# TensorE's order inside an odd half step: the value products ahead of the score unit for the maxima

## The chip, the cores and the metric

The kernel runs on one core of one Trainium2 chip. The metric is the device time of one execution in microseconds (us). The median of three runs of the kernel before is 2089.74 us (2085.26 to 2090.35).

## The reference, cut to what matters

Two transformer layers with adaptive layer norm run over x of shape 8 x 1024 x 128 (eight batches). Layer 0 has a causal attention with one head and a mixture of eight experts. Layer 1 has an attention with 16 heads of width 8 and a feed-forward part. The part around the change is layer 1's attention:

```python
q = jnp.einsum('bnc,hc->bnh', x, Wq).reshape(b, n, m, d)   # m = 16 heads, d = 8
k = jnp.einsum('bnc,hc->bnh', x, Wk).reshape(b, n, m, d)
v = jnp.einsum('bnc,hc->bnh', x, Wv).reshape(b, n, m, d)
weight = jnp.einsum('bimd,bjmd->bmij', q * scale, k * scale)
weight = jax.nn.softmax(weight, axis=-1)
a = jnp.einsum('bmij,bjmd->bimd', weight, v).reshape(b, n, m * d)
```

There are 8 x 16 heads, each with 1024 x 1024 scores, and each row of scores needs its maximum before the exponentials.

## The kernel before, in words

**The units.** Layer 1's scores are computed twice. A *unit of the maximum* (`max_scores`, L613) is a pair of matmuls, one for each head of a pair of heads: 128 queries against 512 keys, 48 rows of bf16 parts. VectorE reduces it to row maxima (`row_max`, L1023). A *unit of the exponential* (`exp_scores`, L623) is the transposed product, 128 keys against 512 queries, with three more rows that bring in the negated maxima. ScalarE takes its exponential into one of four tiles `p` (L810). The *value products* (`values`, L639) are eight matmuls in the profile (four heads and halves in fp32) that multiply the exponentials of two units by v, and add them up in the bank `pv_psum`.

**The half steps.** The main loop counts half steps h. In half step h the exponential's unit h and the maximum's unit h + 32 are filled (LEAD is 16 steps, so the maxima run two pairs of heads ahead). There are 64 pairs of heads and 16 half steps to each, so 1024 half steps. Two half steps, an even one and the odd one behind it, are called a step here. In odd half steps the value products of the step before are issued as well. Every engine runs through the same half steps in its own program.

**The buffers.** All units, of both kinds, take turns in three PSUM buffers of two banks each, in the order exponential h, maximum h + 32, exponential h + 1, and so on. A unit may be filled once the unit three places ahead of it is emptied (`buffer_of`). So exponential h waits for VectorE's reduction of the maximum's unit filled in half step h - 2, and the maximum's unit of half step h waits for ScalarE's exponential of unit h - 1. The value products in odd half step h need the exponentials of the units up to h - 2.

**The rest of the work.** Everything else (layer 0's attention and experts, the projections, the feed-forward part, called *fills* here when they are TensorE's) is cut into stages, and a planner (`lay_out`, L149) puts them into half steps: `ROOM = (13, 4)` gives each even half step 13 and each odd one 4 units of room, `WORK` has each stage's size, and at most one fill goes into a half step. In a half step each engine issues its stages behind its unit. All fills share one bank, `side_psum`; a fill waits until ScalarE (`side_act`) or VectorE (`side_dve`) has emptied the one before. TensorE's program for a half step before the change is:

```python
            if 0 <= h < PAIRS * UNITS:
                exp_scores(h)
            if h + 2 * LEAD < PAIRS * UNITS:
                max_scores(h + 2 * LEAD)
            if h > 1 and h % 2:
                values(h // 2 - 1)
            for name, *at in plan.get(h, ()):
```

The program of TensorE (`tensor_program`, L402) stands here with its helpers. Other lines that the steps below touch: L711 to L800 are ScalarE's stages, L738 its exponential of layer 0 (`exp0`), L928 and L930 VectorE's softmax of layer 0, L852 and L855 the layer norm's statistics, L945 and L951 the search for the largest gate, and L1128 GpSimd's mask.

Of the kernel before, what the change touches and what calls it, by code (L numbers as in the profile page):

```python
# [266 lines left out]
def build(nc, ctx, x_in, Wq0, Wk0, Wvdown, Wvup, Wg, bg, We, be, c0, wmod0,  # L267
# [102 lines left out]
    def halves(half):  # L370

        return slice(4 * half, 4 * half + 4), slice(half * BANK, (half + 1) * BANK)
# [8 lines left out]
    def maxima_in(pair):  # L381
        return S[f"maxima{pair % 2}"], 2 * 16 * (pair // 2 + 1)
# [14 lines left out]
    def rows_of(hh, count):  # L397
        return slice(ROW_HALF * hh, ROW_HALF * hh + count)
# [3 lines left out]
    def tensor_program():  # L402
# [9 lines left out]
        def emptied(*key):  # L412
            u = side[key]
            pe.wait_ge(S["side_" + u.by], u.emptied)
# [186 lines left out]
        def buffer_of(kind, n):  # L601
            buffer, before = unit(kind, n)
            if before:
                pe.wait_ge(S[before[0] + "_done"], before[1] + 1)
            return buffer

        def max_scores(n):
            pair, i, half = n // (2 * T), n // 2 % T, n % 2
            slot, of = pair // GROUP % SLOTS, pair % GROUP
            buffer = buffer_of("max", n)  # L610
            pe.wait_ge(*operands(pair // GROUP))
            for hh in range(2):
                m = e.matmul(buffer[:, hh, :], q_ops[rows_of(hh, K_MAX), slot, of, i * P:(i + 1) * P],  # L613
                             k_ops[rows_of(hh, K_MAX), slot, of, halves(half)[1]], start=True, stop=True)
            m.then_inc(S["max_filled"], 1)

        def exp_scores(n):
            pair, kb, half = n // (2 * T), n // 2 % T, n % 2
            slot, of = pair // GROUP % SLOTS, pair % GROUP
            buffer = buffer_of("exp", n)  # L620
            pe.wait_ge(*maxima_in(pair))
            for hh in range(2):
                m = e.matmul(buffer[:, hh, :], k_ops[rows_of(hh, K_EXP), slot, of, kb * P:(kb + 1) * P],  # L623
                             q_ops[rows_of(hh, K_EXP), slot, of, halves(half)[1]], start=True, stop=True)
            m.then_inc(S["exp_filled"], 1)

        def values(step):
            pair, kb = divmod(step, T)
            b, hp = divmod(pair, HEADS // 2)
            if kb == 0:  # L630
                pe.wait_ge(S["pv_zero"], 1)
                pe.wait_ge(S["pv_copied"], pair)
                emptied("v1", b, 1)
                pe.wait_ge(S["v1_ones"], 2)
            pe.wait_ge(S["exp_done"], 2 * step + 2)
            for hh in range(2):
                for half in range(HALVES):
                    q = 32 * (2 * hh + half)
                    m = e.matmul(pv_psum[q:q + VW, :], v1[b % 2][:, kb, 2 * hp + hh, :], p_sb[(2 * step + half) % 4][:, hh, :],  # L639
                                 start=kb == 0, stop=kb == T - 1)  # L640
            m.then_inc(S["pv_done"], 1)
# [7 lines left out]
        for h in range(-2 * LEAD, PAIRS * UNITS + 2):  # L649
            if 0 <= h < PAIRS * UNITS:  # L650
                exp_scores(h)
            if h + 2 * LEAD < PAIRS * UNITS:
                max_scores(h + 2 * LEAD)
            if h > 1 and h % 2:
                values(h // 2 - 1)
            for name, *at in plan.get(h, ()):
                if name in stages:
                    stages[name](*at)
# [564 lines left out]
    def sync_program():  # L1223
# [132 lines left out]
        for half in range(2):  # L1356
            sp.wait_ge(S[f"out{half}"], 32 * (B // 2))
            sp.wait_ge(S[f"parts{half}"], 16 * PRODUCTS * B)

    tensor_program()  # L1360
    scalar_program()
    vector_program()
# [27 lines left out]
```

## Time and profile before

| what | value |
| --- | --- |
| median of three runs | 2089.74 us |
| the profiled execution's own time | 2084.8 us |
| its span (first to last instruction) | 2083.3 us |
| its mean granted TensorE clock | 0.962 |
| PE busy | 1748.1 us (84%) |
| DVE busy | 1521.8 us (73%) |
| ACT busy | 1354.4 us (65%) |
| POOL busy | 772.0 us (37%) |
| main loop with both kinds of unit | about 237 to 2014 us of the span |

PE is TensorE, PEld its weight loads, DVE VectorE, ACT ScalarE and POOL GpSimd. A busy time counts an engine as busy from the start of an instruction to its modelled end; matmuls overlap, so TensorE's busy time is more than the issue slots that it uses. A wait row says which engine and line sat idle, and whose instruction ended the idle time.

### The profile page before, as it was taken

The page shows a single profiled execution, that of the slowest core. Times are in us where ns is not written, and L with a number is a line of the kernel's source. Part 1 is how long each engine was busy: PE and PEld are TensorE (multiplying, and loading weights), DVE is VectorE, ACT ScalarE, POOL GpSimd, SP SyncE. Part 2 cuts the span into 40 slices and gives each one's busy share as a digit, 9 for nine tenths or more (in the row PEclk, how much of TensorE's full clock was granted, in tenths as well). Part 3 has the DMA queues.
Part 4 walks back from the last instruction along what each step waited for, and adds up shares of the span by engine and source line. Part 5 has one row for each costly group of instructions (what it writes and reads, how often), then busy time and mean ns, then how long its engine had stood idle before and what let it go on. Part 6 is the DMA issues. An engine that isn't in the chain of part 4 may idle for free.

```text
span 2083.3 us, 31153 instructions
## 1 busy us (share of the span) xinstructions
PE 1748.1 (84%) x11854; PEld 666.5 (32%) x11854; DVE 1521.8 (73%) x2300; ACT 1354.4 (65%) x1826; POOL 772.0 (37%) x1127
## 2 busy tenths in 40 slices
PE   5574799988989899998989889898989989777784
PEld 3453332333323243233333333233333333112112
DVE  3435877787777876778768886778868787888861
ACT  2332377766777767776767767776767766766673
POOL 4572245314543164333543155432543243302000
PEclk9886799999999999999999999999999999999997
DMA  2004012112020212002221121302112021301101
GB/s 59 21 21 111 22 40 80 29 38 62 24 86 21 62 54 86 28 20 62 60 63 29 31 61 48 90 20 62 34 33 76 21 59 50 90 20 47 26 15 36
DMA packets 83140, 98.79 MB, mean 47 GB/s; under 512 B 11600, under 2 KB 52784, under 8 KB 82992
## 3 DMA queue, kind: packets, MB, share of 16 engines
q1 hardware_dynamic: 82992, 96.81, 17.0%
q8 instruction: 94, 1.54, 0.3%
q14 instruction: 54, 0.44, 0.1%
HBM read 61.25 MB, written 34.73 MB: 46 GB/s over the span
## 4 chain that ended last, share of the span: by engine, by line
PE 60%; ACT 16%; DVE 12%; POOL 6%; issue 4%; SPq 1%; DMA 1%; ACTq 0%; POOLq 0%; DVEq 0%
PE pv_psum L639 19%; ACT p L810 11%; PE buffer L613 8%; PE buffer L623 8%; DVE row_max L1023 7%; PE side_psum L418 3%; PE side_psum L537 3%; PE side_psum L489 3%; PE side_psum L542 3%; PE side_psum L512 2%; PE side_psum L505 2%; PE side_psum L495 1%; PE side_psum L465 1%; PE side_psum L548 1%; POOL rest L1128 1%
## 5 line engine op out<-in xcount | busy, mean ns | idle before, releaser
L1023 DVE TENSOR_REDUCE row_max<-buffer 128x2 f32<-128x1024 f32 x1024 | 1241.5, 1220 | 339.1 <-PE buffer L613 325.5
L810 ACT ACTIVATE p<-buffer 128x1024 f32<-128x1024 f32 x1024 | 1032.7, 1026 | 328.3 <-PE buffer L623 324.8
L639 PE MATMUL pv_psum<-p,v 128*9 128x512 f32 x4096 | 538.9, 598 | 4.4 <-ACT p L810 3.6
L613 PE MATMUL buffer<-k_ops,q_ops 48*128 48x512 bf16 x2048 | 397.9, 387 | 162.2 <-ACT p L810 130.5
L623 PE MATMUL buffer<-q_ops,k_ops 51*128 51x512 bf16 x2048 | 398.6, 388 | 36.8 <-DVE row_max L1023 34.5
L623 PEld LDWEIGHTS buffer<-q_ops,k_ops 51*128 51x128 bf16 x2048 | 97.4, 93 | 440.9 <-DVE row_max L1023 205.6
L613 PEld LDWEIGHTS buffer<-k_ops,q_ops 48*128 48x128 bf16 x2048 | 99.8, 95 | 268.7 <-ACT p L810 229.6
L1158 POOL TENSOR_SCALAR nm_parts<-nm 128x16 bf16<-128x16 f32 x64 | 13.2, 206 | 401.1 <-DVE nm L972 380.4
L1145 POOL TENSOR_TENSOR hm<-masks,hT_f 128x1024 f32<-128x1024 bf16 x64 | 136.6, 2144 | 57.3 <-PE side_psum L542 48.1
L1128 POOL TENSOR_SCALAR rest<-s 128x128 f32<-128x128 f32 (+3 forms) x64 | 137.1, 2142 | 5.7
L1126 POOL TENSOR_TENSOR s<-s,consts 128x128 f32<-128x128 f32 x64 | 29.2, 456 | 284.2 <-ACT s L732 284.2
L928 DVE CUSTOM_DVE_ANT_0 s<-s,rest 128x128 f32<-128x128 f32 (+3 forms) x64 | 56.1, 876 | 86.5 <-POOL rest L1128 86.5
L639 PEld LDWEIGHTS pv_psum<-p,v 128*9 128x9 f32 x4096 | 60.8, 88 | 163.7 <-issue 151.8
L738 ACT ACTIVATE s<-s,nm 128x256 f32<-128x256 f32 (+3 forms) x64 | 55.2, 863 | 70.8 <-DVE nm L930 70.8
L489 PE MATMUL side_psum<-hT,g 128*128 128x512 f32 (+2 forms) x158 | 72.8, 543 | 2.6
L745 ACT COPY p0T<-side_psum 128x512 f32<-128x512 f32 (+3 forms) x83 | 43.1, 519 | 48.0 <-PE side_psum L495 47.9
L537 PE MATMUL side_psum<-we,hm 128*128 128x128 f32 x448 | 65.8, 290 | 0.0
L542 PE MATMUL side_psum<-we,hm 128*128 128x128 f32 x448 | 64.9, 288 | 0.0
L542 PEld LDWEIGHTS side_psum<-we,hm 128*128 128x128 f32 x448 | 54.2, 191 | 31.0 <-issue 31.0
L495 PE MATMUL side_psum<-consts,s 128*128 128x128 f32 x278 | 49.5, 294 | 10.8 <-ACT s L738 6.7
L732 ACT COPY s<-side_psum 128x256 f32<-128x256 f32 (+3 forms) x79 | 37.7, 477 | 29.2 <-PE side_psum L489 28.3
L537 PEld LDWEIGHTS side_psum<-we,hm 128*128 128x128 f32 x448 | 55.0, 193 | 3.8
(245 smaller groups left out, 1833.6 us busy)
## 6 DMA issues: line engine op xcount, KB each, us to landing
masks<-masks_rows SPq DMA_DIRECT2D x16, 1024.0 KB, 5.6
products<-q_parts SPq DMA_DIRECT2D x48, 256.0 KB, 3.4
products<-k_parts SPq DMA_DIRECT2D x48, 256.0 KB, 3.8
q_ops<-products SPq DMA_DIRECT2D x64, 192.0 KB, 3.4
k_ops<-products SPq DMA_DIRECT2D x64, 192.0 KB, 4.2
attention<-o_sb SPq DMA_DIRECT2D x256, 18.0 KB
x<-in_L_attn_inputs SPq DMA_DIRECT2D x8, 512.0 KB, 3.9
w_sb<-in_L_ffn_W SPq DMA_DIRECT2D x16, 256.0 KB, 3.0
```

What stands on the lines that cost most here:

```text
L418: m = e.matmul(v[:, j * C:(j + 1) * C], weight(j), moving, start=True, stop=True)
L489: e.matmul(v[:, 0:w], g0[:, i * P:(i + 1) * P], hT0[:, at:at + w], start=True, stop=True).then_inc(S["side_filled"], 1)
L495: m = e.transpose(v[:, j * P:(j + 1) * P], s0[i % 2][:, k * P:(k + 1) * P], ident)
L537: e.matmul(o, hm[t % 2][:, k, :], we[:, k, :], start=False, stop=False)
L542: m = e.matmul(o, hm[t % 2][:, k, :], we[:, k, :], start=False, stop=k == EXPERTS - 1)
L613: m = e.matmul(buffer[:, hh, :], q_ops[rows_of(hh, K_MAX), slot, of, i * P:(i + 1) * P], k_ops[rows_of(hh, K_MAX), slot, of, halves(half)[ ...
L623: m = e.matmul(buffer[:, hh, :], k_ops[rows_of(hh, K_EXP), slot, of, kb * P:(kb + 1) * P], q_ops[rows_of(hh, K_EXP), slot, of, halves(half ...
L639: m = e.matmul(pv_psum[q:q + VW, :], v1[b % 2][:, kb, 2 * hp + hh, :], p_sb[(2 * step + half) % 4][:, hh, :], start=kb == 0, stop=kb == T - 1)
L810: e.activation(p_sb[n % 4][:, :, :], unit("exp", n)[0][:, :, :], ACT.Exp).then_inc(S["exp_done"], 1)
L1023: e.tensor_reduce(mx[pair % 2][:, :, i, half], unit("max", n)[0][:, :, :], axis=AX.X, op=ALU.max).then_inc(S["max_done"], 1)
L1128: e.tensor_scalar(rest[:, 0:n], s[:, P:P + n], 0.0, NEG, ALU.is_equal, ALU.mult).then_inc(S["masked"], 1)
L1145: e.tensor_tensor(hm[t % 2][:, :, :], masks[:, :, cols], hT_f[:, cols].unsqueeze(1).broadcast_to([C, EXPERTS, P]), op=ALU.mult).then_inc(S ...
```

## The change

In every half step TensorE's program now issues the value products directly behind the exponential's unit and ahead of the maximum's unit. Even half steps have no value products, so only odd ones differ. No instruction, wait, buffer or other engine's program is added or removed; the order of the units in the three buffers stays the same.

```diff
         for h in range(-2 * LEAD, PAIRS * UNITS + 2):
             if 0 <= h < PAIRS * UNITS:
                 exp_scores(h)
+            if h > 1 and h % 2:
+                values(h // 2 - 1)
             if h + 2 * LEAD < PAIRS * UNITS:
                 max_scores(h + 2 * LEAD)
-            if h > 1 and h % 2:
-                values(h // 2 - 1)
             for name, *at in plan.get(h, ()):
                 if name in stages:
                     stages[name](*at)
```

## Rows read from the trace of the kernel before

**Rows 1.** The page: busy time by engine, share of the span, instructions.

```profile
PE 1748.1 (84%) x11854; PEld 666.5 (32%) x11854; DVE 1521.8 (73%) x2300; ACT 1354.4 (65%) x1826; POOL 772.0 (37%) x1127
```

**Rows 2.** The waits: waiting engine and line, who ended it, total, times, longest.

```profile
PE buffer L613 <- ACT p L810: 130.5, 220, 1.0
...
PE buffer L623 <- DVE row_max L1023: 34.5, 56, 3.5
```

**Rows 3.** Groups by line: the units and value products (busy us, mean ns).

```profile
L1023 DVE TENSOR_REDUCE row_max<-buffer 128x2 f32<-128x1024 f32 x1024 | 1241.5, 1220 | 339.1 <-PE buffer L613 325.5
L810 ACT ACTIVATE p<-buffer 128x1024 f32<-128x1024 f32 x1024 | 1032.7, 1026 | 328.3 <-PE buffer L623 324.8
```

**Rows 4.** Timeline of a step without fills: start us, us, engine, line, operation.

```profile
2006.55 0.39 PE L623 MATMUL buffer<-q_ops,k_ops 51*128 51x512 bf16 x2
...
2007.00 0.38 PE L623 MATMUL buffer<-q_ops,k_ops 51*128 51x512 bf16 x2
2007.04 1.94 ACT L810 ACTIVATE p<-buffer 128x1024 f32<-128x1024 f32 x2 [0.93 <-PE buffer L623]
2007.20 2.58 DVE L1023 TENSOR_REDUCE row_max<-buffer 128x2 f32<-128x1024 f32 x2 [0.29 <-PE buffer L613]
2008.12 0.39 PE L613 MATMUL buffer<-k_ops,q_ops 48*128 48x512 bf16 x2 [0.74 <-ACT p L810]
2008.44 1.05 PE L639 MATMUL pv_psum<-p,v 128*9 128x512 f32 x8
2009.42 0.39 PE L623 MATMUL buffer<-q_ops,k_ops 51*128 51x512 bf16 x2
...
2009.87 0.38 PE L623 MATMUL buffer<-q_ops,k_ops 51*128 51x512 bf16 x2
```

**Rows 5.** Timeline, TensorE: units at which the counted kinds of step begin or end.

```profile
241.68 0.64 PE L613 MATMUL buffer<-k_ops,q_ops 48*128 48x512 bf16 x2
...
244.42 0.39 PE L623 MATMUL buffer<-q_ops,k_ops 51*128 51x512 bf16 x2
...
260.13 0.39 PE L623 MATMUL buffer<-q_ops,k_ops 51*128 51x512 bf16 x2
...
1925.81 0.39 PE L623 MATMUL buffer<-q_ops,k_ops 51*128 51x512 bf16 x2
```

**Rows 6.** Timeline, TensorE in an odd half step with a fill.

```profile
1005.55 0.39 PE L623 MATMUL buffer<-q_ops,k_ops 51*128 51x512 bf16 x2
1005.78 0.38 PE L613 MATMUL buffer<-k_ops,q_ops 48*128 48x512 bf16 x2
1006.09 1.04 PE L639 MATMUL pv_psum<-p,v 128*9 128x512 f32 x8
1007.06 1.16 PE L418 MATMUL side_psum<-wff,hT_b 128*128 128x128 f32 x8
1008.15 0.39 PE L623 MATMUL buffer<-q_ops,k_ops 51*128 51x512 bf16 x2
```

**Rows 7.** Timeline, VectorE and a late maximum's reduction in a stretch without fills.

```profile
949.38 1.21 DVE L1023 TENSOR_REDUCE row_max<-buffer 128x2 f32<-128x1024 f32 x1
...
951.04 1.21 DVE L1023 TENSOR_REDUCE row_max<-buffer 128x2 f32<-128x1024 f32 x1
...
952.30 0.39 PE L623 MATMUL buffer<-q_ops,k_ops 51*128 51x512 bf16 x2 [0.22 <-DVE row_max L1023]
```

**Rows 8.** Timeline, layer 0's negated maximum on VectorE and the exponential that uses it.

```profile
346.45 0.15 DVE L930 TENSOR_SCALAR nm<-mx 128x1 f32<-128x1 f32 x1
...
347.02 0.61 ACT L738 ACTIVATE s<-s,nm 128x384 f32<-128x384 f32 x1
```

**Rows 9.** Stretches: us, busy PE, PEld, DVE, ACT, POOL, PEclk, DMA share, GB/s.

```profile
243.00:2014.00 1771.00, 1567.16 (x10867) 553.71 (x10867) 1390.71 (x1954) 1249.34 (x1635) 649.93 (x975) 0.99 0.18 48
1868.00:2014.00 146.00, 110.84 (x826) 25.77 (x822) 124.89 (x125) 99.93 (x112) 16.94 (x43) 1.00 0.12 30
1061.00:1073.00 12.00, 7.79 (x40) 2.11 (x38) 5.26 (x9) 5.67 (x8) 5.00 (x14) 0.72 0.03 6
```

## The prediction

> **What bounds the kernel now.** I read the page first. TensorE is busy 84% of the span, VectorE 73%, ScalarE 65% [rows 1], so no engine is full, and the question is who waits for whom. In the loop TensorE is busy 1567 of 1771 us [rows 9]; what it idles is mostly one wait. The waits [rows 2] show it: before a maximum's unit (L613) TensorE sat idle 130.5 us in 220 waits for ScalarE, before an exponential's unit (L623) only 34.5 us for VectorE. The timeline shows the round that makes the first wait [rows 4]. In the even half step the exponential's unit starts at 2006.55; ScalarE takes it at 2007.04 and has two of them done 1.94 us later, the first after 1.03 [rows 3, 4]. The next odd half step's maximum's unit needs that buffer and starts only at 2008.12, where 2007.23 would have done: score units follow each other every 0.22 to 0.23 us when nothing holds them (1005.55 to 1005.78 [rows 6]; 2006.55 to 2007.00 is two of them). The value products stand behind this wait though their own exponentials were ready long before. The change lets them run in that hole.
>
> **What the change costs and brings.** No instruction and no semaphore is added: the value products need exponentials up to unit h - 2, for which the even half step's maximum's unit has already waited. So only the order counts. I work it out start to start, with e for the start of the odd exponential's unit.
>
> *Issue slots.* Before: unit to unit 0.23, maximum's unit to value products 0.31 (1005.78 to 1006.09), value products to whatever follows 0.97 to 0.98 (fill or score unit alike) [rows 4, 6]. The next work starts at e + 1.51 plus the wait w. Afterwards: value products at e + x, the maximum's unit 0.98 later, then 0.22 to a score unit or 0.31 to a fill. The step x, from an exponential's unit to value products, is not in the trace. It lies between 0.22 (score unit to score unit) and 0.31 (the other score unit to the same value products); I take 0.31, since both score units have nearly the same shape. So an odd half step without a fill costs 1.51 as before (-0.007), and one with a fill 1.60 (+0.084), because TensorE now goes twice from score units to full-height fp32 matmuls. Counted through the 494 steps from 241.28 to the last maximum's unit, 256 have an odd fill (first half step at 244.42, last at 1925.81) [rows 5]: together **+20 us**. With x at 0.22 the sum would be 0.09 x 494 = 43 us lower; with 0.05 more than 0.31, 25 us higher.
>
> The Trainium skill (TensorE: Matmul & The Clock Gate, The mechanism) says that a weight load is pulled ahead of running matmuls when its row group does not conflict or when it goes to the background weight buffer. By the second half of that rule the load for the value products would hide and x would be near 0.22, with the sum 43 us lower; the 0.31 between units and value products [rows 6] speaks against it.
>
> *The wait that goes.* w is what the odd maximum's unit is later than e + 0.227. It is more than the idle time, since the profile calls TensorE busy for 0.16 us of it. Over the same steps w is above 0.02 in 294 (first at 241.68, last at 2008.12 [rows 4, 5]), and sums to **-175 us**. Check against the waits: 130.5 + 220 x 0.163 = 166 [rows 2], the rest being small ones. Afterwards the unit comes at e + 1.29, where the buffer is free in all but a few steps.
>
> *The wait that comes.* The maximum's unit is now 1.06 - w later, and with it VectorE's reduction: 0.42 us from the unit's start (2006.55 + 0.23) to the reduction's at 2007.20, 1.22 for it, 0.06 (951.04 + 1.21 to 952.30, with rounding) to the next unit, 1.70 in all [rows 3, 4, 7]. The exponential's unit of the next odd half step needs that buffer. Without fills it would be issued 0.22 x 3 = 0.66 after the maximum's unit, and so now waits about 1.04. The round becomes: maximum's unit, reduction (1.70), exponential's unit, 0.31, value products, 0.98, maximum's unit: 2.99 us a step. Before, in rows 4, it was 2009.87 - 2007.00 = 2.87, and 2.79 at best. So a step without any fill gets longer by 0.1 to 0.2, in spite of the hole that is filled. With fills between (0.6 us or more) the new wait shrinks; with two it is nothing. Put step by step into the trace as max(0, maximum's unit's new start + 1.70 - next odd unit's new start), it is there in 183 steps (first before 244.42, 0.04 us; last before 2009.87) and sums to **+132 us**. By kind (w, slots, new wait): no fill in the odd half nor in the next even one, 109 steps (first at 260.13, last at 2007.00 [rows 4, 5]): -79 -1 +94; only the even fill, 129: -34 -1 +30; only the odd, 48: -25 +4 +7; both, 208: -37 +17 +0. First-order sum: -23.
>
> *What is late next.* (a) Where w goes, the following even units come earlier by w and meet ScalarE, whose second exponential still ends when it did (2007.04 + 1.94 = 2008.98 [rows 4], and the unit that needs it would be due at 2008.73), or VectorE. The same step-by-step max over these two gives **+14**. (b) VectorE may be late by itself. Its reductions at 949.38 and 951.04 are 1.66 apart, 0.44 of it other work of its own, and the unit at 952.30 waits for the second [rows 7]. There w is gained and lost again. With each reduction's measured end as a floor the sum rises by 8; part of that end was itself set by waits that go, so I take **+4**. (c) VectorE's stages in odd half steps start up to 1 us later: fills emptied by VectorE that have a fill right behind, +4; three exponentials of layer 0 that come one half step behind their softmax. In such a case the maximum is ready 0.42 us before its use (346.60 and 347.02 [rows 8]), and would now be ready about 0.4 late. Together **+6**. Work on GpSimd and the DMA queues is planned with half steps of slack and is not passed; I cost it at nothing. If it moved, it would be by a fraction of 1 us in each batch, as one wait of 3.5 us a batch for GpSimd's mask, in the stretch at 1061 [rows 9], would take in.
>
> Sum: -175 + 20 + 132 + 14 + 4 + 6 = **+1 us**, against the profiled execution's 2084.8 us. The median shown stands 4.9 us above that execution; the same difference put on it gives 2091 us. About 0.3% (6 us) is what a measurement of this kernel can tell from no change.
>
> **Rivals.**
>
> *The holes are filled and little comes behind (faster).* Terms (a) to (c) are guesses about cover. If they are nothing, 2090 - 23 = 2067; if x also is less than 0.31, each 0.01 takes 5 us more. For it: in the 256 steps with an odd fill the new wait is only 7 us against 62 us of w. Against: spots where VectorE is full anyway [rows 7]. Anything from 2067 to 2083 falls here.
>
> *VectorE becomes the round's bound (slower).* Place: the odd exponential's unit after a late reduction. In those 183 steps VectorE must now idle between its two reductions for about 0.54 us (2.99 - 2 x 1.22), at a fixed place. Its other work, 1391 us less two reductions of 1.22 in each of 495 steps, is 183 us in the loop [rows 3, 9], 0.37 a step, and comes in lumps. A lump above 0.54 lengthens the round by the excess, where before three buffers evened it out. If half of the 183 steps have a lump with 0.25 over, that is +23: 2113. It decides from about 6 us, so already at 25 such steps. For it: VectorE is busy 125 of 146 us in the last stretch [rows 9], where the loop has few fills. Against: many lumps lie in steps with fills.
>
> *The clock falls (slower).* The loop now runs at a granted 0.99 to 1.00 even in the last stretch, where TensorE waits in nearly each step; it fell to the lower of its two levels (1.2 for 2.4 GHz) only after an idle stretch of some 3.5 us [rows 9]. The new waits are about 1 us. If it fell in the last stretch alone, the round of 2.99 would grow by the value products' 1 us and two slots, to 4.2: +55 us, 2145. The Trainium skill (TensorE: Matmul & The Clock Gate, A second HAM failure mode: psum-queue depth-cycling) reports a clock that swings when TensorE idles briefly between groups; this trace has such idling without the swing.
>
> **Chances.** Forecast, within 0.3%: 0.42. Filled holes: 0.27. VectorE's round: 0.29. Clock: 0.02. The range reaches from the faster rival's middle, 2070, to most of the slower one's, 2110; within the forecast's own case it is 2085 to 2096.
>
> **What the changed profile would show.** The wait of L613 for ScalarE nearly gone (130.5 to under 15). L623's wait for VectorE up from 34.5 to some 120 to 160. Steps without fills at 2.99 or just above, from maximum's unit to maximum's unit. An odd half step with a fill like rows 6 at 2.69 instead of 2.60. The last stretch (1868 to 2014) 2 to 6 us longer, the batches in the middle shorter or the same. I am wrong if x is not 0.31, if VectorE sits idle in fewer places than before, or if ScalarE's waits grow by more than tens of us.

## The result and the profile after

The changed kernel takes 2104.5 us (median of five runs, 2100.9 to 2108.6) against 2088.5 us: a ratio of 1.008, 95% interval 1.0061 to 1.0099, so 13 to 21 us slower. The time lies inside the stated range of 2070 to 2110 us, but outside the 0.3% of the forecast, which was no change; the prediction gave this sign 0.31.

The page of the changed kernel, busy time by engine, then the chain (the work that ended last, followed back from the end) by engine and by line:

```profile
span 2102.0 us, 31153 instructions
PE 1767.2 (84%) x11854; PEld 679.9 (32%) x11854; DVE 1503.6 (72%) x2300; ACT 1364.8 (65%) x1826; POOL 775.6 (37%) x1127
...
PE 54%; DVE 27%; POOL 8%; ACT 6%; issue 4%; SPq 1%; DMA 1%; POOLq 0%; ACTq 0%; DVEq 0%
DVE row_max L1023 19%; PE pv_psum L639 17%; PE buffer L623 8%; PE buffer L613 7%; PE side_psum L537 3%; PE side_psum L489 2%; PE side_psum L542 2%; PE side_psum L495 2%; PE side_psum L418 2%; ACT p L810 2%; POOL rest L1128 1%; DVE s L928 1%
```

The chain of the kernel before, by engine:

```profile
PE 60%; ACT 16%; DVE 12%; POOL 6%; issue 4%; SPq 1%; DMA 1%; ACTq 0%; POOLq 0%; DVEq 0%
```

Busy shares are as before [rows 1], and say nothing of why it is slower. The chain does: ScalarE's share fell from 16 to 6% and VectorE's rose from 12 to 27%, of which its reductions are 19% (7% before). The kernel's waits and groups by line (idle time behind the second bar) show what was traded, against rows 2:

```profile
DVE row_max L1023 <- PE buffer L613: 403.3, 445, 18.5
...
PE buffer L623 <- DVE row_max L1023: 152.6, 215, 3.1
```

```profile
L613 PE MATMUL buffer<-k_ops,q_ops 48*128 48x512 bf16 x2048 | 400.5, 389 | 31.3 <-DMA k_ops<-products 21.4 <-DVE row_max L1023 8.2 <-ACT p L810 0.9
L623 PE MATMUL buffer<-q_ops,k_ops 51*128 51x512 bf16 x2048 | 398.4, 388 | 158.7 <-DVE row_max L1023 152.6 <-DMA q_ops<-nm_rows 1.5
```

The maximum's unit waited 130.5 us for ScalarE and now waits 0.9. The exponential's unit waited 34.5 us for VectorE and now waits 152.6, and VectorE itself idles 403 us for its units, in 445 waits, where it idled 325.5 [rows 3], in 491. The timeline of the changed kernel shows the round without fills, TensorE first, then VectorE:

```profile
2022.64 0.39 PE L613 MATMUL buffer<-k_ops,q_ops 48*128 48x512 bf16 x2
2022.86 0.38 PE L623 MATMUL buffer<-q_ops,k_ops 51*128 51x512 bf16 x2
2023.08 0.38 PE L613 MATMUL buffer<-k_ops,q_ops 48*128 48x512 bf16 x2
2024.35 0.39 PE L623 MATMUL buffer<-q_ops,k_ops 51*128 51x512 bf16 x2 [0.89 <-DVE row_max L1023]
2024.67 1.05 PE L639 MATMUL pv_psum<-p,v 128*9 128x512 f32 x8
2025.65 0.39 PE L613 MATMUL buffer<-k_ops,q_ops 48*128 48x512 bf16 x2
```

```profile
2023.07 2.36 DVE L1023 TENSOR_REDUCE row_max<-buffer 128x2 f32<-128x1024 f32 x2 [0.66 <-PE buffer L613]
2026.08 2.36 DVE L1023 TENSOR_REDUCE row_max<-buffer 128x2 f32<-128x1024 f32 x2 [0.66 <-PE buffer L613]
```

From the odd maximum's unit (2022.64) to the next odd exponential's unit (2024.35) are 1.71 us, then 0.32 to the value products and 0.98 to the next maximum's unit: 3.01 a step, where rows 4 had 2.87. VectorE's starts, 3.01 apart, say the same, and its 0.66 us of idle time in each step is the late unit seen from its side.

An odd half step with the fill of rows 6, in the changed kernel:

```profile
1013.84 0.39 PE L623 MATMUL buffer<-q_ops,k_ops 51*128 51x512 bf16 x2
1014.16 1.05 PE L639 MATMUL pv_psum<-p,v 128*9 128x512 f32 x8
1015.14 0.39 PE L613 MATMUL buffer<-k_ops,q_ops 48*128 48x512 bf16 x2
1015.46 1.16 PE L418 MATMUL side_psum<-wff,hT_b 128*128 128x128 f32 x8
1016.55 0.39 PE L623 MATMUL buffer<-q_ops,k_ops 51*128 51x512 bf16 x2
```

It takes 2.71 us instead of 2.60: two turns from score units to full-height matmuls (0.32 each) instead of one.

### The profile page after: what moved, and what is told of

Read it like the earlier page. It is cut to its first block, busy times and chain, and to the rows that moved or that the text cites. A ratio compares the mean times of both kernels' runs of the same rounds, so it can differ in the third digit from the quotient of the medians.

```text
span 2102.0 us, 31153 instructions
## 1 busy us (share of the span) xinstructions
PE 1767.2 (84%) x11854; PEld 679.9 (32%) x11854; DVE 1503.6 (72%) x2300; ACT 1364.8 (65%) x1826; POOL 775.6 (37%) x1127
## 4 chain that ended last, share of the span: by engine, by line
PE 54%; DVE 27%; POOL 8%; ACT 6%; issue 4%; SPq 1%; DMA 1%; POOLq 0%; ACTq 0%; DVEq 0%
DVE row_max L1023 19%; PE pv_psum L639 17%; PE buffer L623 8%; PE buffer L613 7%; PE side_psum L537 3%; PE side_psum L489 2%; PE side_psum L542 2%; PE side_psum L495 2%; PE side_psum L418 2%; ACT p L810 2%; POOL rest L1128 1%; DVE s L928 1%; PE side_psum L548 1%; PE side_psum L505 1%; PE side_psum L512 1%
## 5 line engine op out<-in xcount | busy, mean ns | idle before, releaser
L1023 DVE TENSOR_REDUCE row_max<-buffer 128x2 f32<-128x1024 f32 x1024 | 1226.4, 1218 | 405.1 <-PE buffer L613 403.3
L623 PE MATMUL buffer<-q_ops,k_ops 51*128 51x512 bf16 x2048 | 398.4, 388 | 158.7 <-DVE row_max L1023 152.6
L613 PE MATMUL buffer<-k_ops,q_ops 48*128 48x512 bf16 x2048 | 400.5, 389 | 31.3 <-DMA k_ops<-products 21.4
L613 PEld LDWEIGHTS buffer<-k_ops,q_ops 48*128 48x128 bf16 x2048 | 99.5, 94 | 505.7 <-issue 347.0
L1061 POOL TENSOR_SCALAR xn_f<-x,sm_f 128x128 f32<-128x128 f32 x112 | 52.3, 480 | 10.5 <-DVE k_parts L917 7.0
```

Of the source, the lines that this page charges most:

```text
L1023: e.tensor_reduce(mx[pair % 2][:, :, i, half], unit("max", n)[0][:, :, :], axis=AX.X, op=ALU.max).then_inc(S["max_done"], 1)
```

## The experiments

Theory A: the slowdown is the new round through VectorE, and the time lost depends on which odd half steps are changed. Theory B: it is the extra turns of the last fence. All runs were timed in the same rounds as the kernel before, and every ratio below is to that kernel.

**The change in some odd half steps only.** TensorE's loop gets a condition; `fill(h)` is the planner's size of the fill in half step h.

```diff
+        def fill(at):
+            return sum(work(s) for s in plan.get(at, ()) if s[0] in WORK or s[0].startswith("times_v"))
+
...
+            early = CONDITION
+            if h > 1 and h % 2 and early:
+                values(h // 2 - 1)
             if h + 2 * LEAD < PAIRS * UNITS:
                 max_scores(h + 2 * LEAD)
-            if h > 1 and h % 2:
+            if h > 1 and h % 2 and not early:
                 values(h // 2 - 1)
```

With `fill(h) > 0`:

> Value products ahead of the maximum's unit only in the 257 odd half steps that have a fill; the old order in the other 238. Theory A (the slowdown is the new round: maximum's unit, reduction, next odd exponential's unit, value products): the changed kernel's steps of this kind took 15.5 us less than before and the others 32 us more, so about 2073 us, faster than before. Theory B (the slowdown is the extra turn from score units to full-height matmuls, 0.084 us in each odd half step with a fill): all of these turns are kept and nothing else is, so slower than before, 2100 to 2110 us.

Measured 2069.1 us, ratio 0.989 (0.9877 to 0.9909): faster than before, with every extra turn in it. With `fill(h) == 0`, the complement:

> The complement: value products ahead of the maximum's unit only in the 238 odd half steps without a fill. Theory A: 2088.5 + 32 = about 2120 us, slower than the change itself (2104.5). Theory B: no extra turn at all, so no slower than before, 2088 us or less.

Measured 2111.8 us, ratio 1.010 (1.0085 to 1.0115). It adds no turn and is the slower one. Theory B falls as the whole cause: the turns cost, but the half steps that have them gain all the same, and the loss lies where there are none. A's size was 32 us and came out at about 21. The two halves together (-22 and +21) come to nothing, while the whole change costs 16, so they do not simply add.

With `fill(h) == 0 and fill(h + 1) == 0`, a part of these in which the hole is largest:

> The new order only in the 110 odd half steps with no fill in themselves and none in the next even half step. Here the hole that is filled is the largest (79 us in all) and no turn is added. Theory A (the new round of 2.99 us a step): +24 us as in the changed kernel's own steps of this kind, 2105 to 2115 us, slower than before although the largest holes go. Theory B (turns): no slower than before. Theory C (filling the hole is always a gain, the loss lies in the fills that wait): 40 us or more faster.

Measured 2097.4 us, ratio 1.004 (1.0026 to 1.0055). Slower, as A has it, though 9 us and not 24, below A's range; C is excluded. In its trace the 110 steps themselves, from odd exponential's unit to odd exponential's unit, took 23 us more than in the kernel before, as expected; what A had left out is that the steps around them took 16 us less. Its waits, VectorE's against ScalarE's:

```profile
PE buffer L623 <- DVE row_max L1029: 121.3, 148, 3.8
...
PE buffer L613 <- ACT p L816: 41.3, 87, 1.0
```

(The helper moves line numbers by 6.) In 110 of 495 odd half steps lies more than two thirds of the wait that is new: 121.3 - 34.5 = 87 of 118 us.

With `fill(h - 1) <= 1 and fill(h) + fill(h + 1) >= 6`, a large hole ahead and something between the late unit and the one that needs its buffer:

> The new order only in the 86 odd half steps whose even half step ahead has at most the small fill nm, and which have 6 or more units of fill in themselves or the next even half step together. There the hole for ScalarE is large and the new wait for VectorE small. Theory A: some 60 us of holes go, 20 to 30 come back as waits and turns, so 2050 to 2070 us, the best so far. Theory B: at most 86 x 0.084 = 7 us slower than before.

> The pick of 86 half steps once more, as the base of the wider pick on the same chip: 2050 to 2062 us by either theory.

Measured 2054.9 and 2054.7 us, both times a ratio of 0.984 (0.9823 to 0.9863 and 0.9818 to 0.9868). With 86 of the 495 changes the kernel is 33 to 36 us faster than before. Its waits:

```profile
PE buffer L613 <- ACT p L816: 79.9, 141, 1.0
PE buffer L623 <- DVE row_max L1029: 42.4, 71, 4.3
```

The first is 51 us below that of the kernel before [rows 2], the second only 8 above. Wider, with `fill(h - 1) <= 6`:

> As the pick, but the even half step ahead may have up to 6 units of fill: 155 half steps, 69 more, whose holes sum to 12 us and whose waits and turns come to 5. Theory A: 0 to 7 us less than the pick of 86, which stood at 2055. Theory B: 6 us more than the pick.

Measured 2063.6 us, ratio 0.988 (0.9862 to 0.9896): about 9 us slower than the pick by the medians, where A allowed 0 to 7 faster. The two intervals just touch, so the size is loose. B's turns had 6 us slower, which fits the sign. Start to start, from the pick's trace to this one, the wait at the odd maximum's unit fell from 111.8 to 100.2 us; those at the odd and even exponential's units rose from 38.1 and 26.0 to 46.3 and 31.5, and the turns from score units to full height from 903 to 940. So 12 us of small holes went, as expected, but they brought 14 us of waits and 37 turns of about 0.1 us instead of 5 us in all: A had the costs too small.

**Half a reduction.** VectorE takes the maxima over only half of each unit's columns, in the kernel before and in the changed one.

```diff
-            e.tensor_reduce(mx[pair % 2][:, :, i, half], unit("max", n)[0][:, :, :], axis=AX.X, op=ALU.max).then_inc(S["max_done"], 1)
+            e.tensor_reduce(mx[pair % 2][:, :, i, half], unit("max", n)[0][:, :, 0:BANK // 2], axis=AX.X, op=ALU.max).then_inc(S["max_done"], 1)
```

> The kernel before with VectorE's row maximum taken over only half of each unit's columns (the maxima of the other half are left out), so the reduction falls from 1.22 to about 0.65 us. Both theories: faster than before by the VectorE-bound spots, 2050 to 2085 us; it is the base for the next run.

> The changed kernel with the same half reduction. Theory A: the way from the maximum's unit to the next odd exponential's unit falls from 1.70 to about 1.1 us, so most of the new wait goes while the hole stays filled: at least 50 us faster than its base. Theory B (turns): still 15 to 20 us slower than its base.

Measured 2070.9 us (ratio 0.992, 0.9898 to 0.9934) and 1992.5 us (0.953, 0.9509 to 0.9552). The same change that costs 16 us with a reduction of 1.22 us brings 78 us with one of 0.69:

```profile
L1023 DVE TENSOR_REDUCE row_max<-buffer 128x2 f32<-128x512 f32 x1024 | 693.5, 689 | 782.9 <-PE buffer L613 780.6
...
L623 PE MATMUL buffer<-q_ops,k_ops 51*128 51x512 bf16 x2048 | 398.2, 388 | 58.4 <-DVE row_max L1023 53.0 <-DMA q_ops<-nm_rows 4.0
```

The turns are all there. What went is the wait for VectorE, 152.6 to 53.0 us, while the hole that is filled was even larger in this base (TensorE's idle time for ScalarE before L613: 153.7 us instead of 130.5).

**Half an exponential.** ScalarE takes the exponential over half of each unit's columns; ones stand in for the rest, written once at the start.

```diff
-            e.activation(p_sb[n % 4][:, :, :], unit("exp", n)[0][:, :, :], ACT.Exp).then_inc(S["exp_done"], 1)
+            e.activation(p_sb[n % 4][:, :, 0:BANK // 2], unit("exp", n)[0][:, :, 0:BANK // 2], ACT.Exp).then_inc(S["exp_done"], 1)
...
+        for p in p_sb:
+            e.memset(p[:, :, BANK // 2:BANK], 1.0)
```

> The kernel before with ScalarE's exponential taken over only half of each unit's columns (the other exponentials are left out, ones stand in their place), so it falls from 1.03 to about 0.6 us. The hole before the odd maximum's unit shrinks from 175 us to under 60. Base for the next run; 1980 to 2050 us.

> The changed kernel with the same half exponential. Theory A: there is little hole left to fill, and the new round with VectorE stays, so 60 us or more slower than its base. Theory B: slower than its base by the turns alone, 20 us.

Measured 2014.3 us (0.964, 0.9619 to 0.9664) and 2093.2 us (1.002, 1.0007 to 1.0032): the change costs 79 us here. In the base the hole is down to a third (58 us start to start instead of 175; the first fence has its idle time); in the changed kernel the wait for VectorE is as large as ever (second fence; the two new lines move VectorE's line numbers by 2):

```profile
PE buffer L613 <- ACT p L810: 24.3, 69, 0.6
```

```profile
PE buffer L623 <- DVE row_max L1025: 156.4, 217, 3.1
```

Halving ScalarE's exponential makes the changed kernel only 11 us faster; halving VectorE's reduction made it 112 us faster. So it is VectorE's round that bounds it, and hardly ScalarE.

**The value products ahead of both.**

```diff
+            if h > 1 and h % 2:
+                values(h // 2 - 1)
             if 0 <= h < PAIRS * UNITS:
                 exp_scores(h)
             if h + 2 * LEAD < PAIRS * UNITS:
                 max_scores(h + 2 * LEAD)
-            if h > 1 and h % 2:
-                values(h // 2 - 1)
```

> In every odd half step the value products stand ahead of the exponential's unit as well: values, exponential's unit, maximum's unit. Theory A: the value products leave the round maximum's unit, reduction, next odd exponential's unit (1.70 + 0.23 = 1.93 us), so the odd exponential's unit waits little for VectorE (under 40 us in all) and the odd maximum's unit little for ScalarE; instead the even maximum's unit waits for ScalarE's exponential of the odd one, which is now later. Between 2075 and 2095 us. Theory B: the number of turns is about that before (one per step and one per odd fill, instead of one per step and one per even fill), so the same as before.

Measured 2135.3 us, ratio 1.021 (1.0195 to 1.0224): a miss, 40 us above the range. The wait for VectorE is as small as expected, but the hole has only moved:

```profile
L623 PE MATMUL buffer<-q_ops,k_ops 51*128 51x512 bf16 x2048 | 398.7, 388 | 40.5 <-DVE row_max L1023 36.4 <-DMA q_ops<-nm_rows 3.1
...
L613 PE MATMUL buffer<-k_ops,q_ops 48*128 48x512 bf16 x2048 | 398.4, 387 | 174.5 <-ACT p L810 142.9 <-DMA k_ops<-products 21.6 <-DVE row_max L1023 8.3
```

Start to start, the odd maximum's unit waits 1.3 us (before 175.4) and the even one 193.9 (before 1.1). The reason put forward is that odd half steps hold fewer and smaller fills to stand ahead of it (238 of 494 have none; of the even ones 158); the last run tests it. Without fills this order is the best of the three: the median of the 110 such steps is 2.81 us, against 2.87 before and 3.01 in the changed kernel.

```profile
2038.63 0.39 PE L613 MATMUL buffer<-k_ops,q_ops 48*128 48x512 bf16 x2 [0.68 <-ACT p L810]
2038.95 1.05 PE L639 MATMUL pv_psum<-p,v 128*9 128x512 f32 x8
...
2041.44 0.39 PE L613 MATMUL buffer<-k_ops,q_ops 48*128 48x512 bf16 x2 [0.68 <-ACT p L810]
```

The last run puts the order to use where the odd fill is large: as the pick, but with `fill(h - 1) <= 1 and fill(h) >= 8` (56 of the 86) the value products go ahead of the exponential's unit too.

> The pick of 86 half steps, of which the 56 with a fill of 8 or more units in themselves have the value products ahead of the exponential's unit as well; the other 30 as in the pick. The reason why values_first was slow is taken to be that its hole only moved to the even maximum's unit, which has too little ahead of it where the odd half step has no large fill. If so, the 56 with a large odd fill cost nothing against the pick: 2045 to 2060 us. If the value products ahead of the exponential's unit cost by themselves, by making ScalarE wait, 10 us or more above the pick: 2065 us or more.

Measured 2045.3 us, ratio 0.980 (0.9780 to 0.9813): 2.0% faster than before, and some 6 to 10 us better than the pick, which was timed in other rounds (ratio 0.984). The value products ahead of the exponential's unit cost nothing there, as the reason given above has it. Of all orders tried this is the one to keep. Its waits (its line numbers are moved by 9):

```profile
PE buffer L613 <- ACT p L819: 78.9, 142, 1.0
PE buffer L623 <- DVE row_max L1032: 36.9, 55, 4.3
```

Beside the pick, start to start, the wait at the odd exponential's unit is 29.6 instead of 38.1 us, and everything else about the same.

## Why the mechanism was right and the forecast of no change was not

The sum stood at +1 us; the medians differ by +16. I took both traces apart start to start, from the first odd exponential's unit to the last one that has a maximum's unit behind it, by the prediction's way of counting. The stretch went from 1771.5 to 1788.2 us.

- **The wait that goes.** Expected -175. Measured 175.4 to 1.4 us: right.
- **The wait that comes.** Expected +132. The odd exponential's unit waits 160.9 us instead of 30.2, +131: right, and by kind of step too (no fill +91 for 94, only the even fill +33 for 30, only the odd +7 for 7, both 0). So is the round: 3.01 us against 2.99 expected and 2.87 before. The half reduction and the half exponential show that a change in the size of this wait or of that hole turns the sign or makes the loss five times as large.
- **What is late next.** Expected +24. Even exponential's unit +18, even maximum's unit +4, fills +8: +30. Waits together are -13.4 against -19 expected: by them alone the change would have been faster.
- **Issue slots.** Here the largest part of the miss lies, 10 of 16 us, and this term tips the sum to slower: "I take 0.31" for x, and 0.22 to 0.31 for what follows the maximum's unit, gave +20. The time that is not waiting rose by 30 (1507.5 to 1537.6 us). x measured 0.32, and a maximum's unit to a fill 0.31 to 0.32, so an odd half step with a fill costs 0.107 more instead of 0.084: 256 x 0.107 = 27, and 238 x 0.009 = 2. The profile also has 10 us more at the lower clock in this stretch (29 and 39 us), worth some 5 by my estimate; with it the terms overshoot the 30 by a few us.
- **Outside the sum.** The profiled executions differ by 18.7 us in span, of which 16.7 lie in this stretch. Ahead of it the changed one is 3.9 us later, though nothing there is changed; over the profiles of this study whose program is the same up to there, the stretch starts between 241 and 246 us, so that is scatter. Behind it the changed one is 2 us shorter. Of the five runs the two with granted clocks of 0.961 and 0.963 took 2100.9 and 2103.5 us, the two at 0.957 took 2107.8 and 2108.6: a lower clock goes with a longer single run, by some 5 us.

The Trainium skill (TensorE: Matmul & The Clock Gate, The mechanism) would let the load for the value products hide if it goes to the background weight buffer, with x near 0.22. The changed kernel's trace does not show that, here right behind the exponential's unit of 2024.35:

```profile
2024.67 0.12 PEld L639 LDWEIGHTS pv_psum<-p,v 128*9 128x9 f32 x8 [0.23 <-issue]
...
2025.66 0.10 PEld L623 LDWEIGHTS buffer<-q_ops,k_ops 51*128 51x128 bf16 x2
...
2025.88 0.38 PE L623 MATMUL buffer<-q_ops,k_ops 51*128 51x512 bf16 x2
```

The value products' first load starts at 2024.67 together with its own matmul, and so it does, within 0.02 us, in all 512 groups of value products of both traces. A score unit's load behind another score unit starts 0.22 us ahead of its matmul (2025.66 and 2025.88). Whether the late load is the whole of the 0.10 us of a turn is not shown.

What the changed profile was to show came out for the two waits, for the round, for the odd half step with a fill (2.71 for 2.69) and for the last stretch (+5.8 us, from the first half step of the last batch to the last maximum's unit). The middle did not: of its six batches one got 3.2 us shorter and five 0.3 to 7.5 us longer. One of the prediction's signs of being wrong came true as well: VectorE sits idle for the maximum's units in fewer places than before (445 for 491). That sign was badly chosen, since the idle time itself grew by 78 us, in fewer and longer waits.

So the mechanism was the predicted one, and the sum failed in the size of small terms: gains of 175 us against costs that came to 190 and not 176. Neither cost makes the sign alone: without the new wait or without the turns the sum would be below nothing. A difference of two sums each some thirty times as large as the 6 us in question could not be forecast to the sign from these rows; the chances said so. The rival that gives the sign by lumps of VectorE's other work was not needed. No run tries it by itself, but the kept traces leave it little: over the 110 steps without any fill the mean lies 0.09 us above the median in the changed kernel (3.10 and 3.01) and 0.07 above before (2.94 and 2.87), so longer steps add some 2 us more than they did.

The clock rival is out in the last stretch, for which it was priced: there the clock stayed at 1.00. Stretches of the changed kernel (us, busy PE, PEld, DVE, ACT, POOL, PEclk, DMA share, GB/s):

```profile
1448.00:1451.80 3.80, 2.38 (x20) 0.42 (x16) 3.77 (x8) 2.13 (x3) 2.61 (x6) 1.00 0.58 178
1451.80:1455.20 3.40, 3.40 (x18) 1.10 (x12) 1.65 (x2) 1.31 (x2) 0.56 (x2) 0.50 1.04 263
...
2020.05:2032.11 12.06, 8.67 (x67) 1.81 (x65) 9.43 (x9) 8.33 (x9) 0.00 (x0) 1.00 0.14 46
```

The first two rows qualify this. The prediction read that the clock fell only after an idle stretch of some 3.5 us. In the kernel before it also fell at 840.4 us, after an idle stretch of 1.76 us, and in the changed kernel it fell to its lower level at 1451.8 us, for 3.4 us, where TensorE's last idle stretches were 0.62, 0.90 and 0.52 us, each a wait of an exponential's unit for VectorE. So part of the 10 us more at the lower clock may come from the new wait. One trace cannot tell: over all profiles of this study the loop has 26 to 49 us at the lower clock.

What the prediction missed most was not a term but a reading of its own table by kinds of step. Its terms give -14 us for steps with only the odd fill, -20 with both, -5 with only the even fill and +14 with none. Measured, from odd exponential's unit to odd exponential's unit, are -9, -6, +8 and +24. All but one sign are right, and so the table held the version that beats both kernels.

## What to carry to other kernels

Moving ready work into a wait on an in-order engine also delays what stood behind that wait; follow that one around its buffer's whole round before counting the hole as won. Such a move is worth its place only where the hole is there and something else lies between the delayed unit and the one that needs its buffer, so decide it step by step by what the plan puts around it. When the table by kinds of step has both signs, build the kinds with the good sign instead of the whole.

## What was not expected of the hardware

A size: a turn from a score unit (48 or 51 rows, bf16) to full-height (128-row) fp32 matmuls took 0.32 us start to start in the new order in 467 of 489 places at full clock, where the next score unit would start after 0.22 or 0.23. It is not a property of the new order: in the kernel before the value products also start 0.32 us behind the maximum's unit in 290 places (as at 2008.12 and 2008.44 in rows 4), and 0.31 in 200, of which rows 6 show one. The prediction took the rarer value. On 256 places each 0.007 us of such a misreading is 0.1% of the loop. Turns the other way cost nothing: the value products are followed after 0.98 us by a score unit or by a fill alike. And the clock of the changed kernel fell once (at 1451.8 us) where, from 1436 us on, TensorE's longest idle stretch was 0.90 us.
